# A channel's own input added on VectorE, with the gate, in place of a diagonal product in each sum

## The chip, the cores and the metric

The kernel runs on one core of a Trainium2 chip. The metric is the device time of one execution in microseconds (us), the median of a few runs. The core's engines have short names in the profile: PE is TensorE (matrix products; PEld is its weight loads), DVE is VectorE, ACT is ScalarE, POOL is GpSimd, and SP is the queue that starts the DMAs. They run side by side and wait for each other by semaphores. SBUF is the working memory of 128 partitions, PSUM holds the eight banks that TensorE sums into. All data are 32-bit floats.

## The reference, cut to what matters

Eight sequences of 512 tokens with 256 features pass two layers. The first (attention-like mixing and a mixture of experts) is not touched. The second has a state-space block and then a gated MLP. What the change touches is the end of the state-space block:

```python
h = jax.nn.silu(conv + conv_b)                    # 512 tokens x 512 channels
dA = jnp.exp(dt[..., None] * A)                   # 16 states for each channel
dBu = dt[..., None] * Bmat[:, :, None, :] * h[..., None]
# per token: state = dA * state + dBu ; y = sum over the 16 states of state * C
y = _ssm(dA, dBu, C)
y = y + h * D                                     # the channel's own input, one factor D for each channel
y = y * jax.nn.silu(gate)
return y @ W_out
```

## The kernel before, in words

The second layer works sequence by sequence (b = 0 to 7). 512 channels lie on 128 partitions in KI = 4 tiles (c = 0 to 3), the tokens along the free axis, so one tile of a quantity is 128x512. The scan over tokens is done for one state n and one channel tile c at a time: 16 x 4 = 64 steps s for each sequence. The first 32 steps (the first half) serve tiles 0 and 1 in turn, the last 32 serve tiles 2 and 3. One step is:

- ACT makes exp(dt*A) into one of three PSUM banks (line 1421, `bank<-dt,a_neg`), three steps ahead at most;
- POOL makes dt*h*B (line 1356, `d_in<-u,bc`), from rows `bc` that SP loads for every partition;
- DVE scans (line 1366, `bank<-bank,d_in`) and weighs the states with C (line 1374, `w_st<-bank,bc`);
- PE adds the weighed states to the tile's sum: a product with the identity into the tile's PSUM bank (line 1441, `bank<-w_st,ident`). A product of 32-bit floats runs as two passes, which the profile counts one by one.

The sum of a tile is opened by `begin_output(c)` (lines 1426 to 1433): a product of `skip_diag` (the factors D on a diagonal, made once at lines 497 to 499) with the tile's input `h`, which gives h*D. It waits until the bank has been read by the tile that used it before. After the last step of a half, `gate_output(c)` (lines 1377 to 1380) multiplies the bank by the gate into `hcv` (the buffer that held h), and PE later multiplies all four tiles by `w_out`.

Around this core three other sequences are under way: the front of sequence b+1 (norm, input products, convolution on DVE at lines 1188 and 1192, SiLU, and the step width dt, made by `make_dt` with Abs, Relu, Exp and Ln on ACT), and the MLP of sequence b-1. The MLP has eight up tiles, two hidden layers of eight tiles (PE lines 229 and 230, high and low parts of each operand), and a last product (lines 1674 and 1675). Its weights come by SP into `w_stage` (lines 1510 and 1515) and are cast by ACT into a ring `w_ring` of two slots (line 1597). In the up stage, a cast moves half a slot (128x512), in the hidden layers a whole one (128x1024); SP may load the next weights only when the cast before them is done.

The order of the instructions on each engine is written when the program is built. Each stage of work is a generator that yields a planned time before each piece, and `in_order` lines all stages up by these times, for each engine apart. The planned times are sums of the numbers in `PLAN`, in a model in which a step takes 2.8. They fix only the order; on the chip each engine runs its own list from top to bottom, and waits on semaphores. So an instruction that waits holds up everything behind it on its engine. `dt_first` places `make_dt(0)` on ACT, `up_cast_odd` places the casts of odd weight tiles in the up stage (and with it SP's loads two tiles on, by `mlp_sync`), and `last_add` places the last additions of the MLP on DVE (lines 1581 and 1584).

## Time and profile before

| what | us |
| --- | --- |
| median of 3 runs (2719.23 to 2723.3) | 2720.88 |
| the profiled execution: its own time | 2726.29 |
| the profiled execution: span from first to last instruction | 2724.6 |
| PE busy | 2330.2 |
| DVE busy | 1748.2 |
| ACT busy | 1505.2 |
| POOL busy | 1226.2 |

The span is the length that the rows show; the execution's own time is 1.7 us longer, since it also holds what lies before the first and after the last instruction. The profiled execution is 5.4 us longer than the median of the runs. In rows of time, the first number is the start in us from the span's start, the second the duration, and brackets at a row's end give how long the engine stood idle before it and what ended that. An instruction can start before the one ahead of it on its engine has ended, so starts follow each other more closely than durations.

The second layer begins near 990 us. From the second sequence on, the pattern repeats every 200 to 204 us.

### The profile page before, as it was taken

The page shows a single profiled execution, that of the slowest core. Times are in us where ns is not written, and L with a number is a line of the kernel's source. Part 1 is how long each engine was busy: PE and PEld are TensorE (multiplying, and loading weights), DVE is VectorE, ACT ScalarE, POOL GpSimd, SP SyncE. Part 2 cuts the span into 40 slices and gives each one's busy share as a digit, 9 for nine tenths or more (in the row PEclk, how much of TensorE's full clock was granted, in tenths as well). Part 3 has the DMA queues.
Part 4 walks back from the last instruction along what each step waited for, and adds up shares of the span by engine and source line. Part 5 has one row for each costly group of instructions (what it writes and reads, how often), then busy time and mean ns, then how long its engine had stood idle before and what let it go on. Part 6 is the DMA issues. An engine that isn't in the chain of part 4 may idle for free.

```text
span 2724.6 us, 27484 instructions
## 1 busy us (share of the span) xinstructions
PE 2330.2 (86%) x8452; PEld 1465.7 (54%) x8452; DVE 1748.2 (64%) x2782; ACT 1505.2 (55%) x1982; POOL 1226.2 (45%) x974
## 2 busy tenths in 40 slices
PE   2898989989989846778998998988988988998977
PEld 1456656567566622234554555555555555565666
DVE  3445464555454337899679679689689689687620
ACT  0232433425324225547877876876867866877733
POOL 1232251332422214556556556565556555556622
PEclk6899999999999867888999999998999999999988
DMA  7034534454445533444655645645645544647522
GB/s 227 0 119 137 166 124 133 150 162 132 136 137 155 174 110 108 119 117 131 171 133 131 170 133 134 171 132 129 175 129 134 171 128 138 160 133 176 151 83 78
DMA packets 381907, 374.34 MB, mean 137 GB/s; under 512 B 22369, under 2 KB 308593, under 8 KB 381761
## 3 DMA queue, kind: packets, MB, share of 16 engines
q1 hardware_dynamic: 375616, 355.80, 46.0%
q0 software_dynamic: 6144, 16.79, 2.0%
q8 instruction: 68, 1.11, 0.2%
q14 instruction: 79, 0.64, 0.1%
HBM read 335.45 MB, written 37.06 MB: 137 GB/s over the span
## 4 chain that ended last, share of the span: by engine, by line
PE 20%; DVE 13%; issue 11%; ACT 9%; DMA 6%; POOL 4%; SPq 1%; DVEq 0%; POOLq 0%; ACTq 0%
DMA w_stage<-h_T 5%; PE bank L1441 5%; PE bank L223 4%; DVE bank L1366 4%; PE bank L229 4%; PE bank L230 4%; DVE w_st L1374 4%; POOL d_in L1356 2%; ACT w_ring L1597 2%; ACT bank L1421 2%; DVE cv L1192 2%; ACT L1421 2%; PE bank L1674 1%; POOL f1L L1543 1%; PE bank L1675 1%
## 5 line engine op out<-in xcount | busy, mean ns | idle before, releaser
L1356 POOL TENSOR_TENSOR d_in<-u,bc 128x512 f32<-128x512 f32 x512 | 665.5, 1314 | 452.2 <-DMA bc<-bc_rows 327.7
L1366 DVE TENSOR_TENSOR_SCAN bank<-bank,d_in 128x512 f32<-128x512 f32 x512 | 624.7, 1221 | 185.7 <-ACT bank L1421 156.9
L1441 PE MATMUL bank<-w_st,ident 128*128 128x512 f32 x1024 | 544.8, 646 | 120.2 <-DVE w_st L1374 120.1
L1421 ACT ACTIVATE bank<-dt,a_neg 128x512 f32<-128x512 f32 x512 | 348.4, 687 | 292.9 <-DVE w_st L1374 291.0
L229 PE MATMUL bank<-f1H,w_ring 128*128 128x512 f32 x768 | 355.2, 462 | 34.8 <-POOL f1L L1543 23.8
L1441 PEld LDWEIGHTS bank<-w_st,ident 128*128 128x128 f32 x1024 | 194.2, 201 | 353.9 <-DVE w_st L1374 226.6
L1374 DVE TENSOR_TENSOR w_st<-bank,bc 128x512 f32<-128x512 f32 x512 | 343.9, 673 | 53.0 <-PE bank L1441 52.8
L230 PE MATMUL bank<-f1L,w_ring 128*128 128x512 f32 x768 | 311.3, 405 | 0.0
L229 PE MATMUL bank<-f0H,w_ring 128*128 128x512 f32 x512 | 230.2, 450 | 11.2 <-POOL f0L L1543 5.9
L1597 ACT ACTIVATE w_ring<-w_stage 128x1024 fp32r<-128x1024 f32 (+1 forms) x192 | 173.0, 905 | 112.6 <-DMA w_stage<-h_T 50.9
L1543 POOL TENSOR_TENSOR f0L<-mid,f0H 128x512 fp32r<-128x512 f32 x128 | 170.6, 1334 | 134.6 <-ACT f0H L1626 78.7
L193 POOL TENSOR_TENSOR norm_rstd<-norm_veps,minus_half 128x4 f32<-128x4 f32 x24 | 25.8, 1076 | 429.7 <-DVE norm_veps L189 429.5
L229 PEld LDWEIGHTS bank<-f1H,w_ring 128*128 128x128 f32 x768 | 151.4, 197 | 106.9 <-issue 43.2
L230 PE MATMUL bank<-f0L,w_ring 128*128 128x512 f32 x512 | 208.0, 406 | 0.0
L230 PEld LDWEIGHTS bank<-f1L,w_ring 128*128 128x128 f32 x768 | 151.3, 197 | 52.5 <-issue 23.8
L223 PE MATMUL bank<-f_both,w_s 128*128 128x512 f32 x256 | 140.0, 709 | 33.0 <-DVE s_act L867 33.0
L1421 ACT ACT_TABLE_LOAD x115 | 147.5, 1283 | 2.1
L1543 POOL TENSOR_TENSOR f1L<-mid,f1H 128x512 fp32r<-128x512 f32 x64 | 81.7, 1292 | 128.9 <-ACT f1H L1626 128.8
L223 PE MATMUL bank<-hT,w_in 128*128 128x512 f32 x256 | 125.5, 622 | 11.1 <-ACT f1H L1626 6.8
L229 PEld LDWEIGHTS bank<-f0H,w_ring 128*128 128x128 f32 x512 | 101.6, 199 | 56.2 <-POOL f0L L1543 16.8
L559 DVE TENSOR_REDUCE smax<-bank 128x1 f32<-128x512 f32 x32 | 22.1, 691 | 163.5 <-PE bank L223 163.5
L223 PE MATMUL bank<-e_buf,w_exp 128*128 128x128 f32 x960 | 120.4, 278 | 4.4 <-DMA w_exp<-L_ffn_ew 3.1
(202 smaller groups left out, 3898.5 us busy)
## 6 DMA issues: line engine op xcount, KB each, us to landing
bc<-bc_rows SPq DMA_DIRECT2D x256, 512.0 KB, 5.1
w_stage<-h_T SPq DMA_DIRECT2D x256, 256.0 KB, 3.4
w_exp<-L_ffn_ew SPq DMA_DIRECT2D x240, 256.0 KB, 4.6
w_stage<-w_T SPq DMA_DIRECT2D x128, 128.0 KB, 2.8
eo_rows<-eo SPq DMA_DIRECT2D x56, 256.0 KB, 4.3
xs<-xs_rows SPq DMA_DIRECT2D x24, 512.0 KB, 4.0
xA<-L_attn_x SPq DMA_DIRECT2D x8, 512.0 KB, 6.4
x_mid<-xA SPq DMA_DIRECT2D x8, 512.0 KB, 2.9
```

What stands on the lines that cost most here:

```text
L223: i = pe.matmul(out_, lhs(k), rhs(k), start=(k == 0), stop=(k == nk - 1))
L229: pe.matmul(out_, weights(k), hi(k), start=(k == 0), stop=False)
L230: i = pe.matmul(out_, weights(k), lo(k), start=False, stop=(k == nk - 1))
L1192: dve.scalar_tensor_tensor(out=o, in0=r[:, tap:tap + S], scalar=conv_w[:, tap, c:c + 1], in1=o, op0=ALU.mult, op1=ALU.add).then_inc(tap_ma ...
L1356: pool.tensor_tensor(d_in[:, nth(b, s) % IN, :], u[:, c, :], rows_tile(b, use)[:, 0, :], ALU.mult).then_inc(in_made.sem, 1)
L1366: dve.tensor_tensor_scan(bank[:, :], bank[:, :], d_in[:, nth(b, s) % IN, :], 0.0, ALU.mult, ALU.add).then_inc(scanned.sem, 1)
L1374: dve.tensor_tensor(w_st[:, nth(b, s) % WG, :], state_bank(b, s)[:, :], rows_tile(b, step(s)[2])[:, 1, :], ALU.mult).then_inc(weighed.sem, 1)
L1421: act.activation(state_bank(b, s)[:, :], dt[:, c, :], ACT.Exp, scale=a_neg[:, c, n:n + 1]).then_inc(dA_made.sem, 1)
L1441: pe.matmul(y_bank(c)[:, :], ident[:, :], w_st[:, nth(b, s) % WG, :], start=False, stop=(n == NST - 1)).then_inc(summed.sem, 1)
L1543: pool.tensor_tensor(lo, f_full[:, i % 2, :], hi.bitcast(F32), ALU.subtract).then_inc(low_made.sem, 1)
L1597: act.activation(ring_part(w), stage_part(w), ACT.Copy).then_inc(ring_made.sem, 1)
L1674: pe.matmul(bank[:, j * D:(j + 1) * D], f0H[:, k, token], w3[:, k, :], start=(k == 0), stop=False)
```

## The change

The diagonal product is gone, with `skip_diag`. The first step's product now opens the sum. `gate_output` gets one more DVE instruction: it reads the sum from the bank, adds `h` times D, and writes `y` to SBUF, and the gate is then multiplied in SBUF. The bank is free after the first of the two. `make_dt` loses a semaphore: Exp now waits for the last Relu where it waited for the last Abs. Three numbers of `PLAN` differ.

```diff
-    u_second=8.3, ... dt_first=107, dt_second=2.2,
+    u_second=8.3, ... dt_first=104.9, dt_second=2.2,
-    ... up_cast_even=-0.5, up_cast_odd=6.5, ...
+    ... up_cast_even=-0.5, up_cast_odd=0.5, ...
-    ... up_gate=6.5, last_add=1.5, m_act=9,
+    ... up_gate=6.5, last_add=2.6, m_act=9,
...
-                dve.wait_ge(ssm_weights_in.sem, 7 * 16)
-                for c in range(KI):
-                    dve.tensor_scalar(skip_diag[:, c, :], ident[:, :], d_skip[:, c:c + 1], None, ALU.mult)
...
-                        act.activation(cv[:, c % 2, :], bank[:, :], ACT.Abs, bias=b_dt[:, c:c + 1]).then_inc(abs_made.sem, 1)
+                        act.activation(cv[:, c % 2, :], bank[:, :], ACT.Abs, bias=b_dt[:, c:c + 1])
                         act.activation(dt[:, c, :], bank[:, :], ACT.Relu, bias=b_dt[:, c:c + 1]).then_inc(relu_made.sem, 1)
-                    act.wait_ge(*abs_made.at(b, HC * (half + 1)))
+                    act.wait_ge(*relu_made.at(b, HC * (half + 1)))
...
                 def gate_output(c):
                     dve.wait_ge(*summed.at(b, (c // HC + 1) * HALF))
+
+                    dve.scalar_tensor_tensor(out=y[:, c, :], in0=y[:, c, :], scalar=d_skip[:, c:c + 1], in1=y_bank(c)[:, :],
+                                             op0=ALU.mult, op1=ALU.add).then_inc(y_skipped.sem, 1)
                     dve.wait_ge(*gate_made.at(b, c + 1))
-                    dve.tensor_tensor(y[:, c, :], y_bank(c)[:, :], gate[:, c, :], ALU.mult).then_inc(y_gated.sem, 1)
+                    dve.wait_ge(*y_skipped.at(b, c + 1))
+                    dve.tensor_tensor(y[:, c, :], y[:, c, :], gate[:, c, :], ALU.mult).then_inc(y_gated.sem, 1)
...
                 def begin_output(c):
-                    if c < HC:
-                        pe.wait_ge(*h_made.at(b, c + 1))
-                        if b:
-                            pe.wait_ge(*y_gated.at(b - 1, c + HC + 1))
-                    else:
-                        pe.wait_ge(*y_gated.at(b, c - HC + 1))
-                    pe.matmul(y_bank(c)[:, :], skip_diag[:, c, :], h[:, c, :], start=True, stop=False)
+                    if c >= HC:
+                        pe.wait_ge(*y_skipped.at(b, c - HC + 1))
+                    elif b:
+                        pe.wait_ge(*y_skipped.at(b - 1, c + HC + 1))
...
-                    pe.matmul(y_bank(c)[:, :], ident[:, :], w_st[:, nth(b, s) % WG, :], start=False, stop=(n == NST - 1)
+                    pe.matmul(y_bank(c)[:, :], ident[:, :], w_st[:, nth(b, s) % WG, :], start=(n == 0), stop=(n == NST - 1)
```

What moves is seen in the engines' lists. First DVE, at the end of a sequence's 64 steps, in the steady part; line 1366 is a scan, 1374 a weighing, 1380 the gate, 1581 and 1584 the first of the MLP's two last additions, 1199 and 1204 make dt and u. Before:

```order
L1380 TENSOR_TENSOR hcv<-bank,gate 128x512 [waits gate_made,summed] x2
L1366 SCALAR_TENSOR_TENSOR bank<-bank,d_in 128x512 [waits dA_made,in_made] x2
L1374 TENSOR_TENSOR w_st<-bank,bc 128x512 [waits summed,scanned]
L1366 SCALAR_TENSOR_TENSOR bank<-bank,d_in 128x512 [waits dA_made,in_made]
L1374 TENSOR_TENSOR w_st<-bank,bc 128x512 [waits summed,scanned]
L1581 TENSOR_TENSOR mid<-bank,gbM 128x512 [waits g3_made,last_done]
L1584 TENSOR_TENSOR xM<-xM,mid 128x512 [waits last_scaled]
L1199 TENSOR_TENSOR dt<-dt,cv 128x1024 [waits relu_made,sp_ln]
L1204 TENSOR_TENSOR u<-dt,hcv 128x1024 [waits in_made,h_made,dt_made]
L1366 SCALAR_TENSOR_TENSOR bank<-bank,d_in 128x512 [waits dA_made,in_made]
L1374 TENSOR_TENSOR w_st<-bank,bc 128x512 [waits summed,scanned]
```

The same place now (the lines of the program have shifted by 4 or 3: 1362 is the scan, 1370 the weighing, 1376 the new instruction):

```order
L1376 SCALAR_TENSOR_TENSOR hcv<-hcv,d_skip,bank 128x512 [waits summed]
L1380 TENSOR_TENSOR hcv<-hcv,gate 128x512 [waits y_skipped,gate_made]
L1376 SCALAR_TENSOR_TENSOR hcv<-hcv,d_skip,bank 128x512 [waits summed]
L1380 TENSOR_TENSOR hcv<-hcv,gate 128x512 [waits y_skipped,gate_made]
L1362 SCALAR_TENSOR_TENSOR bank<-bank,d_in 128x512 [waits dA_made,in_made] x2
L1370 TENSOR_TENSOR w_st<-bank,bc 128x512 [waits summed,scanned]
L1362 SCALAR_TENSOR_TENSOR bank<-bank,d_in 128x512 [waits dA_made,in_made]
L1370 TENSOR_TENSOR w_st<-bank,bc 128x512 [waits summed,scanned]
L1578 TENSOR_TENSOR mid<-bank,gbM 128x512 [waits g3_made,last_done]
L1581 TENSOR_TENSOR xM<-xM,mid 128x512 [waits last_scaled]
L1195 TENSOR_TENSOR dt<-dt,cv 128x1024 [waits relu_made,sp_ln]
L1200 TENSOR_TENSOR u<-dt,hcv 128x1024 [waits in_made,h_made,dt_made]
```

Two instructions stand where the gate's two stood before, and two more; nothing else moves down to u. A little further on, the MLP's second pair of last additions stands behind one more scan and weighing than before (`last_add`), still ahead of the first `tokB`.

Second PE, at the middle of a sequence, where the sums of tiles 2 and 3 open; `hT,w_in` is an input product of the next sequence, `hcv,w_x` the product that gives B, C and the rows for dt. Before:

```order
L1441 MATMUL bank<-w_st,ident 128x512 [waits weighed]
L223 MATMUL bank<-hT,w_in 128x512 [waits h_act]
L223 MATMUL bank<-hT,w_in 128x512
L1433 MATMUL bank<-hcv,skip_diag 128x512 [waits y_gated]
L1441 MATMUL bank<-w_st,ident 128x512 [waits weighed]
L1433 MATMUL bank<-hcv,skip_diag 128x512 [waits y_gated]
L1441 MATMUL bank<-w_st,ident 128x512 [waits weighed]
L223 MATMUL bank<-hcv,w_x 96x512 [waits h_act,h_made]
L223 MATMUL bank<-hcv,w_x 96x512 x3
```

Now (1438 is the sum's product):

```order
L1438 MATMUL bank<-w_st,ident 128x512 [waits weighed]
L222 MATMUL bank<-hT,w_in 128x512 [waits h_act]
L222 MATMUL bank<-hT,w_in 128x512
L1438 MATMUL bank<-w_st,ident 128x512 [waits weighed,y_skipped] x2
L222 MATMUL bank<-hcv,w_x 96x512 [waits h_act,h_made]
L222 MATMUL bank<-hcv,w_x 96x512 x3
```

The two diagonal products are gone, and the sum's first products wait for the new DVE instruction.

Third ACT, right behind that place: `xp` is the copy of those rows, 1421 the exponential of a step, 1234 to 1239 make dt, 1597 is a cast of MLP weights. Before:

```order
L1272 ACTIVATE xp<-bank 96x512 [waits dt_done,bc_stored1,xp_done]
L1421 ACTIVATE bank<-dt,a_neg 128x512 [waits weighed] x2
L1234 ACTIVATE cv<-bank,b_dt 128x512 [waits u_made,dA_made,dt_done]
L1235 ACTIVATE dt<-bank,b_dt 128x512
L1234 ACTIVATE cv<-bank,b_dt 128x512 [waits u_made,dA_made,dt_done]
L1235 ACTIVATE dt<-bank,b_dt 128x512
L1237 ACTIVATE cv<-cv 128x1024 [waits abs_made]
L1239 ACT_TABLE_LOAD
L1239 ACTIVATE cv<-cv 128x1024 [waits sp_exp]
L1421 ACT_TABLE_LOAD
L1421 ACTIVATE bank<-dt,a_neg 128x512 [waits weighed]
L1597 ACTIVATE w_ring<-w_stage 128x1024 [waits h_done,stage_in1,stage_in0]
```

Now (1230 to 1235 make dt, 1594 is the cast):

```order
L1268 ACTIVATE xp<-bank 96x512 [waits dt_done,bc_stored1,xp_done]
L1421 ACTIVATE bank<-dt,a_neg 128x512 [waits weighed]
L1230 ACTIVATE cv<-bank,b_dt 128x512 [waits u_made,dA_made,dt_done]
L1231 ACTIVATE dt<-bank,b_dt 128x512
L1230 ACTIVATE cv<-bank,b_dt 128x512 [waits u_made,dA_made,dt_done]
L1231 ACTIVATE dt<-bank,b_dt 128x512
L1233 ACTIVATE cv<-cv 128x1024 [waits relu_made]
L1235 ACT_TABLE_LOAD
L1235 ACTIVATE cv<-cv 128x1024 [waits sp_exp]
L1421 ACT_TABLE_LOAD
L1421 ACTIVATE bank<-dt,a_neg 128x512 [waits weighed] x2
L1594 ACTIVATE w_ring<-w_stage 128x1024 [waits h_done,stage_in1,stage_in0]
```

One exponential has moved from ahead of dt to behind it (`dt_first`). In the up stage of the MLP, each cast of an odd weight tile stands right behind the even one's, or one exponential behind it, where it stood some six units of the plan later (`up_cast_odd`): the cast of tile 3 is ahead of the first SiLU, those of tiles 5 and 7 each ahead of the SiLU that they followed, and the loads of the weights on SP move up with them, past one load of `bc` rows and the store of the result.

## Rows read from the trace of the kernel before

**Rows 1.** The page: busy time of the engines, and shares of the chain that ended last.
```profile
PE 2330.2 (86%) x8452; PEld 1465.7 (54%) x8452; DVE 1748.2 (64%) x2782; ACT 1505.2 (55%) x1982; POOL 1226.2 (45%) x974
...
PE 20%; DVE 13%; issue 11%; ACT 9%; DMA 6%; POOL 4%; SPq 1%; DVEq 0%; POOLq 0%; ACTq 0%
```

**Rows 2.** Windows: stretch and length in us, busy us of PE, PEld, DVE, ACT, POOL (instructions), PE clock, DMA.
```profile
1799.00:1877.00 78.00, 67.13 (x239) 41.36 (x237) 76.93 (x106) 52.02 (x69) 42.64 (x33) 0.93 0.46 117
1747.00:1798.00 51.00, 49.90 (x171) 32.97 (x172) 34.77 (x39) 40.60 (x52) 35.51 (x29) 0.97 0.61 166
1708.00:1744.00 36.00, 34.77 (x110) 20.28 (x110) 19.77 (x23) 32.44 (x42) 16.55 (x14) 1.00 0.61 174
```

**Rows 3.** All waits of VectorE from 1799 to 1877 us: total, times, longest.
```profile
DVE tokB L1405 <- PE bank L223: 0.3, 1, 0.3
```

**Rows 4.** The chain of waits where a sequence's steps end: start, us, what.
```profile
1801.93 0.86 PE bank L1433 x2
```

**Rows 5.** VectorE in order of time, where the second layer starts.
```profile
986.48 0.87 DVE L499 TENSOR_SCALAR skip_diag<-ident,d_skip 128x128 f32<-128x128 f32 x4
993.74 0.43 DVE L181 BATCH_NORM_STATS2 normB_stat<-xB 128x6 f32<-128x256 f32 x1 [6.39 <-DMA xB<-x_mid]
```

**Rows 6.** VectorE in order of time, from the end of a sequence's steps.
```profile
1798.06 1.29 DVE L1380 TENSOR_TENSOR hcv<-bank,gate 128x512 f32<-128x512 f32 x2 [5.29 <-PE bank L1441]
1799.26 2.33 DVE L1366 TENSOR_TENSOR_SCAN bank<-bank,d_in 128x512 f32<-128x512 f32 x2
...
1812.68 0.69 DVE L1405 TENSOR_TENSOR tokB<-bank,gaB 128x512 f32<-128x512 f32 x1
1813.40 0.69 DVE L1408 TENSOR_TENSOR xM<-xM,tokB 128x512 f32<-128x512 f32 x1
1814.01 1.23 DVE L1366 TENSOR_TENSOR_SCAN bank<-bank,d_in 128x512 f32<-128x512 f32 x1
```

**Rows 7.** VectorE, 1799 to 1877 us, groups: count, busy us, mean ns, idle us.
```profile
L1192 DVE SCALAR_TENSOR_TENSOR cv<-raw,conv_w,cv 128x512 f32<-128x512 f32 x6 | 6.4, 1064 | 0.0
...
L198 DVE TENSOR_SCALAR cv<-xB,normB_stat,normB_rstd 128x256 f32<-128x256 f32 x4 | 4.5, 1178 | 0.0
L1564 DVE SCALAR_TENSOR_TENSOR mid<-bank,sc_in,mid 128x512 f32<-128x512 f32 x6 | 4.4, 736 | 0.0
```

**Rows 8.** VectorE in the last sequence, 38 us behind the same place.
```profile
2443.95 1.23 DVE L1366 TENSOR_TENSOR_SCAN bank<-bank,d_in 128x512 f32<-128x512 f32 x1 [1.51 <-POOL d_in L1356]
```

**Rows 9.** VectorE behind the middle of a sequence.
```profile
1715.37 1.23 DVE L1366 TENSOR_TENSOR_SCAN bank<-bank,d_in 128x512 f32<-128x512 f32 x1 [5.39 <-ACT bank L1421]
```

**Rows 10.** TensorE at the middle of a sequence.
```profile
1710.37 1.02 PE L1433 MATMUL bank<-hcv,skip_diag 128*128 128x512 f32 x2
...
1713.80 3.60 PE L223 MATMUL bank<-hcv,w_x 128*96 128x512 f32 x8
1718.08 1.98 PE L223 MATMUL bank<-xp,w_dt 64*128 64x512 f32 x4 [0.68 <-ACT xp L1272]
```

**Rows 11.** ScalarE at the middle of a sequence.
```profile
1710.96 1.33 ACT L1216 ACTIVATE hcv<-cv,conv_b 128x512 f32<-128x512 f32 x2
...
1715.81 1.04 ACT L1597 ACTIVATE w_ring<-w_stage 128x1024 fp32r<-128x1024 f32 x1
1717.43 0.59 ACT L1272 ACTIVATE xp<-bank 96x512 f32<-96x512 f32 x1 [0.58 <-PE bank L223]
...
1718.93 0.69 ACT L1421 ACTIVATE bank<-dt,a_neg 128x512 f32<-128x512 f32 x1 [0.33 <-DVE w_st L1374]
```

**Rows 12.** ScalarE in the last MLP, where the hidden layers begin.
```profile
2624.54 1.06 ACT L1597 ACTIVATE w_ring<-w_stage 128x1024 fp32r<-128x1024 f32 x1 [0.72 <-DMA w_stage<-h_T]
```

**Rows 13.** The convolution's instruction over the whole span: shortest, median, longest in ns.
```profile
L1192 DVE SCALAR_TENSOR_TENSOR cv<-raw,conv_w,cv x96: 731/746/1870, 1007.5 to 2306.8; 128x512 f32<-128x512 f32 x96
```

**Rows 14.** GpSimd in order of time, where a sequence's steps end.
```profile
1800.63 2.54 POOL L1356 TENSOR_TENSOR d_in<-u,bc 128x512 f32<-128x512 f32 x2 [2.84 <-DVE bank L1366]
```

**Rows 15.** The norm's application over the whole span, columns as in rows 13.
```profile
L198 DVE TENSOR_SCALAR cv<-xB,normB_stat,normB_rstd x32: 400/1347/1503, 997.0 to 2242.6; 128x256 f32<-128x256 f32 x32
```

More of the change, by code:

```diff
@@ L27 @@
     rows_out=106.9, norm_rstd=29, norm_stats=26, norm_apply=34.2, conv=45.7, raw_gap=11.7, tap_gap=3, u_first=136.5,
-    u_second=8.3, hT_act=36.9, raw_act=42.3, h_first=66, h_second=97, rows_act=102, dt_first=107, dt_second=2.2,
+    u_second=8.3, hT_act=36.9, raw_act=42.3, h_first=66, h_second=97, rows_act=102, dt_first=104.9, dt_second=2.2,
     gate_second=23.1, turn=35.2, raw_pe=38.6, gate_pe_first=92, rows_pe=100, dt_pe_first=98, dt_pe_second=-5.4,
     gate_pe_second=17, rows_in=3.3, input=3.2, weigh=-10.6, out_add=13.6, decay=3.7, sum=5.6, out_pe=10.8, up_gap=9,
-    hid_gap=13.8, mlp=20, up=14, hid=3.6, up_cast_even=-0.5, up_cast_odd=6.5, hid_cast_even=8, hid_cast_odd=12.6,
-    stage=3.1, m_rstd=1.9, m_low=10.9, up_low=11.6, hid_low=10.5, m_apply=5, up_gate=6.5, last_add=1.5, m_act=9,
+    hid_gap=13.8, mlp=20, up=14, hid=3.6, up_cast_even=-0.5, up_cast_odd=0.5, hid_cast_even=8, hid_cast_odd=12.6,
+    stage=3.1, m_rstd=1.9, m_low=10.9, up_low=11.6, hid_low=10.5, m_apply=5, up_gate=6.5, last_add=2.6, m_act=9,
     up_act=2.2, hid_act=8, m_turn=3.3, up2_pe=1.3, hid_pe_odd=3.5, last_pe=-1.1)
@@ L162, in adaln_kernel @@
         a_neg = keep("a_neg", [P, KI, NST])
-        skip_diag = keep("skip_diag", [P, KI, P])
         s3_row = keep("s3_row", [P, D])
@@ L1091, in adaln_kernel @@
             xp_done, xp_made = signal("xp_done"), signal("xp_made")
-            dt_done, abs_made, relu_made = signal("dt_done", KI), signal("abs_made", KI), signal("relu_made", KI)
+            dt_done, relu_made = signal("dt_done", KI), signal("relu_made", KI)
             sp_exp, sp_ln, dt_made, u_made = (signal(n, HALVES) for n in ("sp_exp", "sp_ln", "dt_made", "u_made"))
@@ L1096, in adaln_kernel @@
                                                           ("dA_made", "in_made", "scanned", "weighed", "summed"))
-            y_gated = signal("y_gated", KI)
+            y_skipped, y_gated = signal("y_skipped", KI), signal("y_gated", KI)
             so_done, so_gated, xM_made = (signal(n, 2) for n in ("so_done", "so_gated", "xM_made"))
```

## The prediction

> **What bounds the kernel now.** I began with the page's busy times and chain shares [rows 1]: TensorE is busy for 86% of the span and VectorE for 64%, yet TensorE holds only 20% of the chain that ended last, and VectorE 13%. So no one engine sets the time. I then cut one steady sequence into stretches and read the busy time of each engine in each [rows 2], with the waits beside it. Three stretches come out.
>
> In the first, some 78 us from the end of a sequence's 64 steps, VectorE works 76.93 of 78 us, and its waits there come to 0.3 us in all [rows 3]; TensorE has 11 us to spare. Here each instruction that VectorE gains moves the end. The same stretch stands at the start of each of the seven sequences that follow another.
>
> The second stretch is the middle of a sequence with the first hidden layer behind it: TensorE works 34.77 of 36 us and ScalarE 32.44, while VectorE works 19.77. The third is the second hidden layer: TensorE works 49.90 of 51 us, up to the end of the steps.
>
> So the change takes from TensorE, which binds in the second and third stretch, and gives to VectorE, which binds in the first. What counts is where the removed and the added instructions stand: a pair at the end of each sequence, ahead of a VectorE-full stretch, and a pair at its middle, in the second stretch. None stands in the third.
>
> **What is removed.** The two passes of a diagonal product take 0.86 us on the chain [rows 4], so 0.43 us a pass. There are 8 sequences with 4 products of two passes: 64 x 0.43 = 27.5 us of TensorE's work, 1.72 us for each of the 16 pairs. If all of it shortened the chain, the time would fall by 27.5 us: the lower bound. Making `skip_diag` took 0.87 us once. It goes at no gain, because VectorE next waits 6.39 us for a load [rows 5], which waits for a store that does not need it. The moved wait for Relu in place of Abs costs nothing: Relu follows Abs on the same engine, and the Exp that waits is behind both on it.
>
> **What is added.** Two gates start the next instruction 1.20 us later (1798.06 to 1799.26), so 0.60 us each; two independent instructions on VectorE start 0.61 us apart (1813.40 to 1814.01), and one that reads the last one's result starts 0.72 us behind it (1812.68 to 1813.40) [rows 6]. The new instruction is of the form scalar_tensor_tensor with one input in PSUM and one in SBUF, like line 1564's, which takes 736 ns where a plain one takes 690 [rows 7, 6]. I take 0.72 + 0.05 = 0.77 us from its start to that of the gate that waits for it, and 0.61 from there to the next. A pair takes 2 x (0.77 + 0.61) = 2.76 us in place of 1.20: 1.56 us more. For 16 pairs that is 25 us of VectorE's work, and if all of it lengthened the chain, it would be the upper bound.
>
> **At a sequence's end (seven times).** The pair ends 1.56 us later, and the scan behind it starts later. Of that, the stretch's 0.3 us of waits can absorb 0.3 [rows 3], so 1.26 us reach its end. The 1.72 us saved on TensorE bring nothing here: the diagonal products stood where TensorE was waiting for VectorE's first weighing anyway, since a scan and a weighing follow the gates. Now TensorE waits 1.7 us there instead, and the bank's earlier release serves a sum that is not ready. In the last such stretch VectorE waits 1.51 us for GpSimd [rows 8]; that can hold most of the 1.56, and I put 0.3 there. Sum: 6 x 1.26 + 0.3 = +7.9 us. Behind the eighth sequence there is no such stretch, and the last MLP hides the pair. That pair and the place of the last additions (the MLP's second pair goes behind one scan and one weighing, all within the same full stretch, and TensorE waits for none of it there) I put at 0.
>
> **At a sequence's middle (eight times).** VectorE's 1.56 us are covered: a few instructions on, a scan waits 5.39 us for an exponential [rows 9]. If that cover were gone, they would cost 1.56 each. TensorE reaches `w_x` 1.72 us earlier, but that product needs h, which ScalarE makes at 1710.96 + 1.33 = 1712.29; it starts now at 1713.80 [rows 10, 11], so it can gain 1.51. Its reader, the copy `xp`, now waits 0.58 us behind a cast that ends at 1815.81 + 1.04 = 1816.85 (and starts at 1717.43), so `xp` can gain 0.58. Behind it an exponential with a wait of 0.33 us goes behind dt [rows 11], where its operand is long ready: 0.33 more at best, 0.91 in all, and then TensorE's dt products, which wait 0.68 us for `xp` today [rows 10], follow. At worst it is 0, since the casts and loads of the hidden layer run behind one another. I take 0.4, near the middle: 8 x 0.4 = -3.2 us.
>
> **Casts and loads moved ahead in the up stage.** SP's weight loads pass one load of `bc` rows and a store, and ScalarE's casts pass a SiLU. In the steady sequences they lie in the VectorE-full stretch, where ScalarE works 52.02 of 78 us [rows 2]; I put 0. In the last MLP, ScalarE waits 0.72 us for a load where the hidden layers begin [rows 12]; an earlier load can take that, -0.7 us, and 0 at worst.
>
> **The sum.** 7.9 - 3.2 - 0.7 = +4.0 us. The profiled execution took 2726.3 us, so it becomes 2730.3; the median of the runs is 5.4 us lower, and so is the forecast: 2724.9, called 2725.
>
> **A rule that speaks against the change.** The convolution's instruction reads two operands in SBUF and takes 731 ns when alone, up to 1870 when not [rows 13]. The old gate read PSUM and SBUF; the new one reads `hcv` and `gate`, both in SBUF. The Trainium skill ("SBUF — State Buffer", section "Who interferes with whom") says that a VectorE instruction with two SBUF inputs contends with a GpSimd instruction that reads SBUF, the second to come blocking for the whole of the other, and that one with a single SBUF input does not. By that rule the trace's 731 and 1870 agree, and the new gate would be exposed where the old one was not. With one GpSimd product of 1.27 us waited for at each of the seven ends the sum would be +4.0 + 8.9 = +12.9 us by the rule, and +4.0 without it.
>
> **The rivals.**
> *Slower: the new gate collides.* A product of GpSimd takes 2.54 / 2 = 1.27 us, and just ahead of 1800.63 GpSimd idles for 2.84 us [rows 14], so the gates at 1798 to 1800.8 start in its idle time; that speaks against a collision. But VectorE's new schedule is 1.56 us longer, so its last gate reaches the point where GpSimd starts again, unless GpSimd, which waits for VectorE's scan there, moves along. With one collision of 1 us at each of seven ends: +7, so 2732. From 0.2 us per end the time is above the bound of no change.
> *Faster: fewer collisions.* Within a VectorE-full stretch the convolution's six instructions take 1064 ns against 731 alone, and the norm's four 1178 against 400 [rows 7, 13, 15]: 6 x 0.33 + 4 x 0.78 = 5.1 us lost per stretch, 36 us over seven. These depend on which instructions meet, and the moved gates, loads and casts lay all of them anew. A third less would be -12 us: 2713. A third more is equally open in principle; the slower rival and the range hold it.
> *Faster: TensorE is the true bound at the middle.* It works 34.77 of 36 us there. If h were early and each pair's 1.72 us came through in full, 8 x 1.72 = 13.8 in place of 3.2 gives 2725 - 10.6 = 2714. Against it stands the order h, `w_x`, `xp`, in which ScalarE's cast sets the start.
> *Slower: adjacent casts hold ScalarE.* Two casts in a row wait for a load that has only just been asked for, and the exponentials behind them are late. ScalarE has 26 us to spare in each VectorE-full stretch, which speaks against it; it decides from the point where VectorE's scans wait for an exponential there. With 1.4 us, two exponentials of 0.69, at each of seven sequences: +10, 2735.
>
> **How the numbers follow.** A difference below 0.2%, 5.4 us, cannot be told from no change for this kernel; the bounds are 2715.4 and 2726.3. The forecast gets 0.44 (its own range 2719 to 2731: 0.05 faster, 0.24 same, 0.15 slower), fewer collisions 0.20 (0.15 faster, 0.05 same), TensorE at the middle 0.13 (0.10, 0.03), the gate's collision 0.15 (0.02 same, 0.13 slower), the casts 0.08 (0.01, 0.07). Together: faster 0.30, same 0.35, slower 0.35. The range that leaves out 2 in 10 reaches from 2709 to 2737.
>
> **What the profile of the changed kernel would show.** Right: 32 new instructions near 0.74 us and 32 gates near 0.69; the first scan 2.76 us behind the first of them at a sequence's end; TensorE waiting some 1.7 us for the first weighing there; still hardly a wait on VectorE in the 78 us behind; a period per sequence longer by about 0.9 us. Wrong: gates above 0.75 us (the collision); the convolution's mean in that stretch far from 1064 ns (the other collisions); the period shorter with TensorE's waits at the middle unchanged (TensorE was the bound); casts with waits of over 1 us in the up stage.

## The result, and the profile after

The changed kernel takes 2737.29 us (median of 4 runs, 2733.26 to 2742.31), beside 2720.12 us of the kernel before on the same chip: ratio 1.0062, 95% interval 1.0043 to 1.0081. It is slower, by three times the 0.2% that the prediction took as the least difference that can be told. The forecast was 2725 us; the measured time lies at the upper end of the stated range (2737), 0.3 us beyond it, and on the side to which the prediction gave a chance of 0.35. The forecast was 4 us of change and 17 were measured: that the time comes so near the range is due to the range, which was held open for collisions that no term priced.

From the page of the changed kernel: span and instructions, busy times, shares of the chain that ended last.

```profile
span 2731.5 us, 27400 instructions
...
PE 2298.4 (84%) x8388; PEld 1447.5 (53%) x8388; DVE 1776.5 (65%) x2810; ACT 1505.9 (55%) x1982; POOL 1236.6 (45%) x974
...
PE 17%; DVE 16%; issue 11%; ACT 9%; DMA 7%; POOL 3%; SPq 1%; DVEq 0%; POOLq 0%; ACTq 0%
```

TensorE has 64 passes fewer than before and works 32 us less; VectorE has 28 instructions more (32 added, the four of `skip_diag` gone) and works 28 us more [rows 1]. VectorE's 28 us are not the price of the change alone: the added instructions take 23.8 us, the gates 2.8 more than before and the MLP's norm 11.2 more, while one group of the first layer (`qk_tok<-qk_tok,os_row_t`), which the change does not touch, happens to take 10.1 less in this trace. TensorE's share of the chain fell from 20 to 17%, VectorE's rose from 13 to 16%.

The spans of the two profiled executions differ by only 6.9 us, where the medians differ by 17. One row shows where the rest is: VectorE's first instruction of the second layer.

```profile
983.72 1.40 DVE L180 BATCH_NORM_STATS2 normB_stat<-xB 128x6 f32<-128x256 f32 x4 [7.17 <-DMA xB<-x_mid]
```

In the execution of before it started at 993.74 [rows 5], 10 us later, though ahead of it the change took out only the 0.87 us of `skip_diag`. From that instruction to the end the kernel before took 2724.6 - 993.7 = 1730.9 us, the changed one 2731.5 - 983.7 = 1747.8: 16.9 us more, close to the difference of the medians. The traces are therefore compared by this length, called "layer 2" below; a trace is one execution, a verdict rests on the runs.

The three stretches (columns as in [rows 2]), and all waits of VectorE in the first of them:

```profile
1799.00:1880.00 81.00, 64.84 (x226) 39.43 (x225) 79.42 (x108) 51.90 (x67) 44.11 (x34) 0.94 0.44 112
1747.00:1796.00 49.00, 47.70 (x169) 31.59 (x170) 34.52 (x39) 39.51 (x51) 35.23 (x29) 1.00 0.62 172
1708.00:1744.00 36.00, 33.90 (x106) 19.36 (x106) 21.69 (x25) 32.69 (x43) 17.24 (x14) 1.00 0.60 176
```

```profile
DVE tokB L1405 <- PE bank L222: 0.9, 2, 0.6
```

The first stretch, as I cut it, grew from 78 to 81 us and VectorE is as full as it was (76.93 of 78 before [rows 2]). The second, at a sequence's middle, holds 0.9 us less of TensorE's work, and the third, up to the end of the steps, is 49 us long in place of 51; they did not become the problem.

To see where in a sequence the time is lost, I took the start of every scan (steps 0 to 63) and compared each kernel with the one before, averaged over the sequences 1 to 6. A positive number is us lost between the two steps, and step 64 is the next sequence's first. Steps 0 to 12 hold the MLP's last additions and its norm, 32 to 40 the middle, 60 to 64 the gates at the end:

```
kernel                     0-12  12-32  32-40  40-60  60-64   whole
changed kernel              1.8   -0.5    1.3   -1.5    1.7     2.8
casts put back (e1)         1.7   -0.2    0.9   -1.4    1.5     2.5
arithmetic only (e2)        0.3   -0.1    0.2   -0.3    1.4     1.4
order only (e3)             2.1    0.3    1.4   -1.1   -0.3     2.4
last_add only (e8)          1.8    0.2    0.4   -0.3   -0.1     2.0
no product, no sum (e4)     0.1   -0.7    0.2    0.0   -0.3    -0.7
tiles 0, 1 on VectorE (e5)  0.2    0.2    0.0   -0.4   -0.3    -0.4
tiles 2, 3 on VectorE (e6)  0.3    0.2    0.4   -0.3    1.5     2.2
in first weighed (e7)       0.0    0.3    1.0    0.0   -0.1     1.2
extra work at end (e9)      2.1   -0.3    0.0    0.1    2.9     4.7
extra work at middle (e10)  0.7   -0.2    0.2   -0.2   -0.2     0.3
last_add put back (e11)     2.3    0.7    0.9   -0.9    1.3     4.2
both covered (e12)         -0.3    0.1    0.0    0.7   -0.3     0.1
```

The changed kernel loses 2.8 us per sequence: 1.7 at the end's gates and 1.8 at the norm, and between step 12 and 60 it gains 0.7.

**The end.** VectorE in order of time, the place of [rows 6]:

```profile
1796.86 0.75 DVE L1376 SCALAR_TENSOR_TENSOR hcv<-hcv,d_skip,bank 128x512 f32<-128x512 f32 x1 [5.40 <-PE bank L1438]
1797.71 0.69 DVE L1380 TENSOR_TENSOR hcv<-hcv,gate 128x512 f32<-128x512 f32 x1
1798.32 0.74 DVE L1376 SCALAR_TENSOR_TENSOR hcv<-hcv,d_skip,bank 128x512 f32<-128x512 f32 x1
1799.17 0.69 DVE L1380 TENSOR_TENSOR hcv<-hcv,gate 128x512 f32<-128x512 f32 x1
1799.78 2.34 DVE L1362 TENSOR_TENSOR_SCAN bank<-bank,d_in 128x512 f32<-128x512 f32 x2
```

The first scan starts 2.92 us behind the first added instruction; before, it stood 1.20 us behind the first gate. The added instruction takes 0.75 us (forecast: near 0.74), but what waits for it starts 0.85 us behind it, not 0.77. TensorE now waits for the first weighing, 2.19 us where some 1.7 were forecast:

```profile
1802.84 1.32 PE L1438 MATMUL bank<-w_st,ident 128*128 128x512 f32 x2 [2.19 <-DVE w_st L1370]
```

**The norm.** VectorE, GpSimd and SP where the MLP's norm is applied, in the kernel before. The three fences are the three engines; SPq rows are DMAs that SP issues.

```profile
1824.62 1.80 DVE L198 TENSOR_SCALAR mid<-xM,normM_stat,normM_rstd 128x256 f32<-128x256 f32 x4
1826.34 1.22 DVE L1366 TENSOR_TENSOR_SCAN bank<-bank,d_in 128x512 f32<-128x512 f32 x1
```

```profile
1824.04 1.26 POOL L1356 TENSOR_TENSOR d_in<-u,bc 128x512 f32<-128x512 f32 x1
1826.62 2.50 POOL L1356 TENSOR_TENSOR d_in<-u,bc 128x512 f32<-128x512 f32 x2 [1.31 <-DMA bc<-bc_rows]
```

```profile
1820.76 0.88 SPq L1510 DMA_DIRECT2D w_stage<-w_T  x2
1821.68 10.56 SPq L1335 DMA_DIRECT2D bc<-bc_rows  x3
```

The same in the changed kernel:

```profile
1825.74 3.69 DVE L197 TENSOR_SCALAR mid<-xM,normM_stat,normM_rstd 128x256 f32<-128x256 f32 x4
1829.36 1.22 DVE L1362 TENSOR_TENSOR_SCAN bank<-bank,d_in 128x512 f32<-128x512 f32 x1
```

```profile
1825.16 3.80 POOL L1352 TENSOR_TENSOR d_in<-u,bc 128x512 f32<-128x512 f32 x3
```

```profile
1813.74 0.46 SPq L1331 DMA_DIRECT2D bc<-bc_rows  x1
...
1818.53 7.69 SPq L1331 DMA_DIRECT2D bc<-bc_rows  x2
```

Before, SP asks for the `bc` rows at 1821.68. They arrive 4.94 us later, so GpSimd stands idle until 1826.62, and by then the norm's four instructions are over: they end at 1826.42. That is a gap of 0.2 us; in the sequences 2 to 6 GpSimd starts from 0.3 us ahead of the norm's end to 0.4 behind it. In the changed kernel the rows were asked for at 1818.53, 7.2 us ahead of the norm in place of 2.9; GpSimd runs three products on end, and the four instructions take 3.69 us in place of 1.80. Over the whole span, shortest, median and longest in ns:

```profile
L198 DVE TENSOR_SCALAR mid<-xM,normM_stat,normM_rstd x32: 399/402/1451, 1217.6 to 2602.6; 128x256 f32<-128x256 f32 x32
```

```profile
L197 DVE TENSOR_SCALAR mid<-xM,normM_stat,normM_rstd x32: 400/830/1348, 1210.6 to 2612.9; 128x256 f32<-128x256 f32 x32
```

The sum over the group's 32 instructions goes from 17.9 to 29.1 us, 11.2 us more, all of it in VectorE-full stretches. The first of the four takes 0.83 us at every end in both kernels. What is new is that the second and third take 1.35 us each: in the kernel before at one of seven ends, in the changed one at all seven. In the sequences 1 to 6 that makes 1.9 us for each, as much as step 0 to 12 loses.

**The middle** went as forecast in its rows. In this sequence the middle's first gate instruction starts at the same time in both traces (1706.97 us before, 1706.98 now), so the times can be compared as they stand: `xp` on ScalarE no longer waits for TensorE and stands 0.66 us earlier (1717.43 to 1716.77), and Abs on dt's rows 1.0 us earlier (1719.56 to 1718.56) [rows 11]. Two rows of ScalarE, two of VectorE:

```profile
1716.77 0.57 ACT L1268 ACTIVATE xp<-bank 96x512 f32<-96x512 f32 x1
...
1718.56 0.69 ACT L1230 ACTIVATE cv<-bank,b_dt 128x512 f32<-128x512 f32 x1 [0.64 <-PE bank L222]
```

```profile
1709.28 1.12 DVE L1380 TENSOR_TENSOR hcv<-hcv,gate 128x512 f32<-128x512 f32 x1
...
1715.37 1.23 DVE L1362 TENSOR_TENSOR_SCAN bank<-bank,d_in 128x512 f32<-128x512 f32 x1 [3.26 <-ACT bank L1421]
```

The second gate of the pair takes 1.12 us here, where an operation of GpSimd still runs (`f1L<-mid,f1H`, two of them from 1708.58 to 1711.52), and 0.69 at the end. VectorE then still waits 3.26 us, so the longer gate is covered. From step 12 to 60 the changed kernel gains 0.7 us in sum.

### The profile page after: what moved, and what is told of

It reads as the page before. It is cut to its first block, busy times and chain, and to the rows that moved or that the text cites. A ratio compares the mean times of both kernels' runs of the same rounds, so it can differ in the third digit from the quotient of the medians.

```text
span 2731.5 us, 27400 instructions
## 1 busy us (share of the span) xinstructions
PE 2298.4 (84%) x8388; PEld 1447.5 (53%) x8388; DVE 1776.5 (65%) x2810; ACT 1505.9 (55%) x1982; POOL 1236.6 (45%) x974
## 4 chain that ended last, share of the span: by engine, by line
PE 17%; DVE 16%; issue 11%; ACT 9%; DMA 7%; POOL 3%; SPq 1%; DVEq 0%; POOLq 0%; ACTq 0%
DMA w_stage<-h_T 6%; PE bank L1438 5%; DVE bank L1362 5%; DVE w_st L1370 4%; PE bank L228 4%; PE bank L229 4%; PE bank L222 3%; POOL d_in L1352 2%; ACT w_ring L1594 2%; ACT bank L1421 2%; ACT L1421 2%; DVE cv L1188 2%; POOL f1L L1540 1%; DVE mid L197 1%; DVE mid L1561 1%
```

## The experiments

Ratios are to the kernel before on the same chip, with 95% intervals. The diffs are against the kernel before, unless said otherwise.

**e1, one number of the plan put back in the changed kernel.**

```diff
-    up_cast_odd=0.5
+    up_cast_odd=6.5
```

> The changed kernel with one number of the plan put back (up_cast_odd 6.5). Theory 1: with the casts moved ahead, SP asks for the bc rows about 3 us sooner, GpSimd's products of that stretch then run while VectorE applies the MLP's norm, and two of its four instructions take 1.35 us instead of 0.40; 11 us of the 17 us lost are this. Then the four take 0.83, 0.40, 0.40, 0.40 again (the group's sum falls from 29 to about 18 us) and the time is near 2726 us, ratio to before 1.002. Theory 2: the collision comes from the 1.5 us by which VectorE is late behind the two added instructions, whatever SP does; then the sum stays near 29 us and the time near 2737, ratio 1.006.

Measured: 2745.84 us, ratio 1.0074 [1.0058, 1.0090]. The norm's instructions stay long (their sum is 27.2 us):

```profile
L197 DVE TENSOR_SCALAR mid<-xM,normM_stat,normM_rstd x32: 400/829/1349, 1221.5 to 2622.7; 128x256 f32<-128x256 f32 x32
```

Theory 1 as I put it falls: the moved casts alone are not the cause. Theory 2 (VectorE's lateness) would explain it, and e2 and e3 decide on it.

**e2, the change without the three numbers of the plan.** The diff is against the changed kernel.

```diff
-    dt_first=104.9 ... up_cast_odd=0.5 ... last_add=2.6
+    dt_first=107 ... up_cast_odd=6.5 ... last_add=1.5
```

> The change without the three numbers of the plan. Theory 1: the same as with the casts alone put back, 2726 us, ratio 1.002, made of seven ends of a sequence at 1.1 to 1.4 us each less 3 us at the middles. Theory 2: 2737 us, ratio 1.006. If dt_first and last_add were worth something of their own, this run stands above the one with only the casts put back, by their worth.

Measured: 2739.07 us, ratio 1.0052 [1.0036, 1.0069]; layer 2 1741.6 us, +10.8.

```profile
L197 DVE TENSOR_SCALAR mid<-xM,normM_stat,normM_rstd x32: 399/402/1349, 1218.4 to 2615.7; 128x256 f32<-128x256 f32 x32
```

The median is 402 ns again, the sum 19.7 us. So VectorE's lateness does not make the collision at five of the seven ends (at the last two it is there): theory 2 falls in the main, and the collision comes from the order. The time hardly falls, though: the arithmetic alone still costs 0.52%, 1.4 us at each end.

**e3, the order without the arithmetic.** The diff is e2's in reverse, on the kernel before.

> The kernel before with the three new numbers of the plan, the diagonal product kept. Theory 1: the norm's application meets GpSimd's products here too, +11 us, near 2731, ratio 1.004. Theory 2: no collision without the added VectorE work: 2718 to 2721, ratio 1.000 or a little below.

Measured: 2739.30 us, ratio 1.0049 [1.0032, 1.0065], layer 2 +11.8. The group's sum is 29.1 us:

```profile
L198 DVE TENSOR_SCALAR mid<-xM,normM_stat,normM_rstd x32: 401/832/1350, 1221.6 to 2618.9; 128x256 f32<-128x256 f32 x32
```

The order alone costs as much as the arithmetic alone, and it costs it at the norm (2.1 us from step 0 to 12). The two do not add up to the changed kernel: 0.52% and 0.49% against 0.62% [0.43, 0.81]. The table has the place. Between step 12 and 60 the changed kernel gives back 0.7 us per sequence, where e2 gives back 0.2 and e3 loses 0.6, so 1.1 us are there only when both are made; in the other columns the differences cancel. The rows at the middle point the same way: e2 has `xp` 0.66 us earlier and dt where it was, e3 has `xp` as before and dt 0.3 us earlier, and only both together have dt 1.0 us earlier. That this is the cause of the whole 1.1 us is not shown.

**e4, no diagonal product, and nothing in its place** (h*D is left out of the result).

```diff
-                    pe.matmul(y_bank(c)[:, :], skip_diag[:, c, :], h[:, c, :], start=True, stop=False)
...
-                    pe.matmul(..., start=False, stop=(n == NST - 1)
+                    pe.matmul(..., start=(n == 0), stop=(n == NST - 1)
```

> The kernel before without the diagonal product and with nothing in its place: h*D is left out of the result. It prices TensorE's 27.5 us alone. As forecast: nothing at the ends of a sequence, where TensorE waits for VectorE, and 0.4 us at each middle: 2717, ratio 0.999. Rival, TensorE is the bound at the middle: 1.72 us each, 2706, ratio 0.995. The lower bound, all of it on the path: 2693.

Measured: 2716.16 us, ratio 0.9960 [0.9945, 0.9974]. The 27.5 us of TensorE are worth about 11 us, between my value and the rival's; the trace shows -6.0 in layer 2. In this order of the instructions it is what a way of doing this sum off TensorE could bring if VectorE's part cost nothing.

**e5, tiles 0 and 1 on VectorE** (the pair at the middle), **e6, tiles 2 and 3 on VectorE** (the pair at the end). The plan is before's; only the set differs:

```diff
+ON_VECTOR = (0, 1)      # e6: (2, 3)
...
+                    if c in ON_VECTOR:
+                        dve.scalar_tensor_tensor(out=y[:, c, :], in0=y[:, c, :], scalar=d_skip[:, c:c + 1], in1=y_bank(c)[:, :], ...)
...
+                    if c not in ON_VECTOR:
                         pe.matmul(y_bank(c)[:, :], skip_diag[:, c, :], h[:, c, :], start=True, stop=False)
```

> Before's plan; tiles 0 and 1 get h*D on VectorE with the gate (the pair at a sequence's middle), tiles 2 and 3 keep the diagonal product. Theory 'the place decides': the added pair lies under VectorE's wait of 5 us at the middle, so it costs nothing, and the product that goes stood at the end of a sequence, where TensorE waits: 0 to -5 us, 2720 to 2726 beside 2725 of before, ratio 0.998 to 1.000. Rival 'every added instruction counts': half of the 14 us of the arithmetic alone, ratio 1.0026.

> The other half: tiles 2 and 3 get h*D on VectorE (the pair at a sequence's end, ahead of the VectorE-full stretch), tiles 0 and 1 keep the diagonal product. Theory 'the place decides': all of the cost of the arithmetic alone is here, +12 to +15 us, ratio 1.0045 to 1.0055. Rival: half of it, ratio 1.0026.

Measured: e5 2722.86 us, ratio 0.9981 [0.9964, 0.9997]; e6 2732.85 us, ratio 1.0019 [1.0005, 1.0032]. The signs are those of "the place decides": the pair at the middle costs nothing, and e5's interval leaves out the rival's 1.0026; the pair at the end does cost. The size of e6 is short of what was expected, +5 us in the runs and not 12 to 15: its interval leaves out the expected 1.0045 and holds the rival's 1.0026, so e6 alone does not decide between the two. Its own trace has layer 2 14.4 us longer and 1.5 us lost at each end as in e2, but the profiled execution is the slowest of its twelve (2741.07 us; they spread over 14 us). In the traces the halves add up to the whole (-4.4 and +14.4 us in layer 2, e2 +10.8); in the runs they do not (-0.19% and +0.19%, e2 +0.52%). Why is open; e9 and e10 test the place with more weight.

**e7, h*D added to the first weighed states.** Tiles 2 and 3 only, at the middle; the gates stay as before.

```diff
+                    dve.tensor_tensor(w, state_bank(b, s)[:, :], rows_tile(b, step(s)[2])[:, 1, :], ALU.mult ...)
...
+                    if first:
...
+                        dve.scalar_tensor_tensor(out=w, in0=y[:, c, :], scalar=d_skip[:, c:c + 1], in1=w, ...)
```

> Before's plan; for tiles 2 and 3 h*D is added on VectorE to the first weighed states, right at a sequence's middle, where VectorE has idle time, and TensorE's product for them goes; tiles 0 and 1 keep the diagonal product, which stands where TensorE waits. The gates stay as before. If the place decides, this has TensorE's gain at the middle and none of VectorE's cost at the end: 2718 to 2724 beside 2725, ratio 0.997 to 0.9995. If the first weighed states come too late for TensorE by the added 0.75 us each, 1.000 to 1.002.

Measured: 2733.58 us, ratio 1.0026 [1.0013, 1.0039]. It is slower: the "too late" branch, and a little beyond it. Shortest, median and longest of the added instruction:

```profile
L1382 DVE SCALAR_TENSOR_TENSOR w_st<-hcv,d_skip,w_st x16: 750/752/1662, 1118.2 to 2506.2; 128x512 f32<-128x512 f32 x16
```

It reads two operands in SBUF and takes up to 1.66 us. It stands on the way from scan to sum, and 1.0 us per sequence is lost from step 32 to 40, though less work is asked of TensorE there.

**e8, last_add alone.**

```diff
-    last_add=1.5
+    last_add=2.6
```

> The kernel before with last_add 2.6 and nothing else. In the run with the casts put back (where the collision stayed) one weighing stands ahead of the MLP's last addition, and SP asked for the bc rows 4.98 us ahead of the norm's application where it was 2.94 before, so GpSimd's products ran beside it. If last_add does that, the group of the MLP's norm takes 27 to 29 us here instead of 18, and the time is 7 to 11 us above before: ratio 1.0025 to 1.004. If it takes dt_first or the added instructions as well, the group stays at 18 and the ratio at 1.000.

Measured: 2733.99 us, ratio 1.0026 [1.0012, 1.0040]; the group's sum is 27.2 us. VectorE at the norm, GpSimd, SP:

```profile
1829.21 3.69 DVE L198 TENSOR_SCALAR mid<-xM,normM_stat,normM_rstd 128x256 f32<-128x256 f32 x4
```

```profile
1828.63 3.80 POOL L1356 TENSOR_TENSOR d_in<-u,bc 128x512 f32<-128x512 f32 x3
```

```profile
1822.60 0.88 SPq L1510 DMA_DIRECT2D w_stage<-w_T  x2
1823.53 6.17 SPq L1335 DMA_DIRECT2D bc<-bc_rows  x2
```

One number that moves a weighing ahead of an addition lets SP ask for the rows 5.7 us ahead of the norm (1823.53 to 1829.21) and no longer 2.9; nothing else in the kernel differs. The weighing acts on that ask through SP's queue, in two steps. An earlier `bc` load (1812.57 before, 1815.84 in e8) waits for the weighing that frees its buffer, 7.2 us before and 5.8 in e8; the weight load that stands ahead of the ask waits for a cast of weights that came in behind that `bc` load, 5.0 us before and 2.1 in e8. From the second end on, the ask comes 21.6 to 22.4 us behind the sequence's first scan in the kernel before, 19.6 to 21.2 in e8 and 18.1 to 18.8 in the changed kernel.

The traces of the two kernels, e1, e2, e3, e8 and e11 hold 49 ends of a sequence. Where SP asked 4.6 us or more ahead of the norm, the second and third instruction of the norm took about 1.35 us, every time; where it asked 3.6 us or less ahead, never; the one end between (3.7, in the kernel before) has them too. That settles the mechanism: the norm was spared this only because GpSimd was short of its rows at that moment.

**e9, more work at each end; e10, the same at each middle.** The gate is computed three times. Both kernels also let Exp wait for Relu in place of Abs, as the change does, and use that semaphore for the repeated gates (not in the cut below):

```diff
+                    if c in (2, 3):     # e10: (0, 1)
+                        for i in range(2):
+                            dve.tensor_tensor(y[:, c, :], y_bank(c)[:, :], gate[:, c, :], ALU.mult).then_inc(again.sem, 1)
+                            dve.wait_ge(*again.at(b, 2 * (c % HC) + i + 1))
```

> Before's arithmetic and plan; at each sequence's end the gate of tiles 2 and 3 is computed three times in place of once, each waiting for the one ahead of it: 4 more VectorE instructions of 0.72 us, 2.9 us per end, about 1.7 times what the change adds there. Theory 'VectorE's time at the end is on the path': 7 x 2.9 = 20 us less what waits absorb, so +15 to +20 us, ratio 1.0055 to 1.0075. Rival 'the loss is in the alignment, not in the added time': under +7 us, ratio under 1.0025.

> The same four extra instructions at each sequence's middle (tiles 0 and 1), 2.9 us in each of eight places, ahead of a wait of VectorE of 5.4 us. As forecast the wait covers them: 0 to +3 us, ratio 1.000 to 1.001. Rival 'every added instruction counts': +20 us, ratio 1.0075.

Measured: e9 2754.89 us, ratio 1.0100 [1.0077, 1.0122], so +27 us; e10 2730.34 us, ratio 1.0008 [0.9993, 1.0023], not to be told from nothing. VectorE at an end in e9:

```profile
1812.62 1.42 DVE L1382 TENSOR_TENSOR hcv<-bank,gate 128x512 f32<-128x512 f32 x2 [5.38 <-PE bank L1445]
1814.07 0.69 DVE L1384 TENSOR_TENSOR hcv<-bank,gate 128x512 f32<-128x512 f32 x1
1814.68 1.41 DVE L1382 TENSOR_TENSOR hcv<-bank,gate 128x512 f32<-128x512 f32 x2
1816.12 0.69 DVE L1384 TENSOR_TENSOR hcv<-bank,gate 128x512 f32<-128x512 f32 x1
1816.73 2.34 DVE L1366 TENSOR_TENSOR_SCAN bank<-bank,d_in 128x512 f32<-128x512 f32 x2
```

The first scan starts 4.11 us behind the first gate, 2.91 us more than before. In the table the end loses 2.9 us, which is all of it, and another 2.1 us go by step 12: the norm's four instructions take 0.9 us more per sequence (the group has grown by 5.3 us over the span), and `tokB` waits 0.9 us more for TensorE. So VectorE's time at an end is paid in full, with 1.8 us per sequence on top; at a middle the runs show no cost. This is the clearest of the results.

**e11, the changed kernel with last_add put back.**

```diff
-    last_add=2.6
+    last_add=1.5
```

> The changed kernel with last_add put back to 1.5; the casts stay ahead. If last_add alone makes GpSimd's products meet the MLP's norm, the group of the norm falls from 29 to about 18 us and the ratio to before to 1.003 to 1.005. If the casts ahead do it too (SP then asks for the bc rows without waiting for a cast), it stays at 27 to 29 us and the ratio at 1.005 to 1.0065.

Measured: 2750.11 us, ratio 1.0078 [1.0054, 1.0103].

```profile
L197 DVE TENSOR_SCALAR mid<-xM,normM_stat,normM_rstd x32: 400/830/1350, 1224.9 to 2636.1; 128x256 f32<-128x256 f32 x32
```

The collision stays, at all seven ends, though this kernel's `last_add` is that of before. With e8, either of the two moves, the last additions or the casts and loads, brings the rows in time for it. (e11 also keeps `dt_first`, which no run tests alone.) And with one of them put back the changed kernel is no faster (e1, e11).

**e12, both additions where VectorE has idle time.** e5, and for tiles 2 and 3 e7's addition in their eleventh step, in the second hidden layer; no diagonal product is left.

```diff
+                    late = n == 10 and c >= HC
```

> Before's plan, no diagonal product at all. Tiles 0 and 1 get h*D with the gate at the middle, tiles 2 and 3 get it in the weighed states of their eleventh step, in the second hidden layer, where VectorE works 34.77 of 51 us and TensorE is full. The gates at a sequence's end stay as before. If TensorE's time is worth what leaving the product out gave (ratio 0.996) and both places are covered: 2716 to 2720 beside 2726, ratio 0.996 to 0.998. If the two added instructions delay the sums as they did in the first weighed states, 1.000 to 1.002.

Measured: 2730.61 us, ratio 1.0015 [1.0000, 1.0031].

```profile
L1382 DVE SCALAR_TENSOR_TENSOR w_st<-hcv,d_skip,w_st x16: 750/767/1614, 1172.4 to 2556.8; 128x512 f32<-128x512 f32 x16
```

From step 40 to 60 it loses 0.7 us per sequence, and the whole comes to +0.1 where leaving the product out gave -0.7 (e4). My reading is that VectorE's idle time in that stretch is waiting inside the chain of scan, weighing and sum, so an instruction put between two links makes what follows late; the two of 0.75 us cost 0.7 us together, and no run tests them apart.

The version that is faster than the kernel before is e5, by 0.2% [0.0, 0.4]: it moves h*D of tiles 0 and 1 only.

## Why the prediction was right or wrong

- **That the place decides what VectorE's time costs:** right, and shown. e9 and e10 put the same 2.9 us at either place: +1.00% and +0.08%.
- **The added pair, +1.56 us:** 1.72 us. What depends on the new instruction starts 0.85 us behind it. No wait absorbs a part of it (VectorE's waits are 0.9 us in that stretch in place of 0.3). So 1.7 us come through where the forecast had 1.26, some 3 us over seven ends; in e2 it is 1.4.
- **"The 1.72 us saved on TensorE bring nothing here":** doubtful. Leaving all products out gains 0.40% (e4), which is 11 us where my terms for the product hold 3.2, so 8 us are missing; whether they come from the ends or the middles, e4 does not tell. In e5 it is this product that goes, and the kernel gains 0.19%, but e5 also puts h*D of the middle's pair on VectorE, which changes when those banks come free, so it doesn't isolate the product.
- **The middle, -3.2 us:** the step is right in its rows (`xp`'s wait of 0.58 us gone, dt 1.0 us earlier), and 0.7 us per sequence are gained between steps 12 and 60, against 0.4 forecast. The prediction writes the cast's start there as 1815.81 and its end as 1816.85; the row has 1715.81 [rows 11], so the end is 1716.85. The 0.58 is read from the row's bracket and stands.
- **"That pair and the place of the last additions (...) I put at 0":** this is the step that failed, together with the zero for the casts and loads moved ahead in the steady sequences. Moving one weighing ahead of an addition costs 0.26% alone (e8), the three numbers 0.49% (e3). The reason given, that all lies in the same full stretch and TensorE waits for none of it, looked at the wrong reader. The weighing frees a buffer for a `bc` load of SP, the loads behind that one in SP's queue come sooner, and the next `bc` load sets when GpSimd runs beside VectorE's norm. The 11.2 us at the norm are most of the distance between the forecast's +4.0 us and the measured +17.
- **The rivals:** of the collisions the prediction had the size and the mechanism (5.1 us lost per stretch, laid anew by the moves), but gave a chance only to fewer of them, and left more of them to the range. It named the convolution and the norm of `xB`. The one that came is that of the MLP's norm, which had it at one of seven ends before and was in none of the rows that I read. The gate's own collision came about at the middle (1.12 us), where it is covered, and not at the end. That adjacent casts hold up VectorE's scans does not show in the stretch read: VectorE waits 0.9 us in all of it, for TensorE.

The Trainium skill ("SBUF — State Buffer", section "Who interferes with whom") says more than I used: one SBUF input keeps a VectorE instruction clear of GpSimd only outside the modes that use two ports, and tensor_scalar is among the operations that can enter such a mode. The trace agrees that the form is exposed: the norm's instruction, with one large SBUF input, takes 0.40 us alone and 1.35 us when it falls behind the start of a GpSimd product of 1.3 us.

## What to carry to other kernels

Price an instruction by its place: the same 2.9 us of VectorE's work cost 27 us over the kernel in front of a stretch in which VectorE is full, and nothing that the runs can tell in front of a wait. When the order is touched, follow each moved instruction to the buffer that it frees, to the load that waits for the buffer, and to the engine that the load wakes; then look at what that engine will run beside. An instruction that is fast in the trace may be so by a few tenths of a microsecond of luck, and a list of what would be slow if its neighbour came earlier belongs in the range.

## What the hardware showed that I had not expected

- A dependent VectorE instruction behind the three-operand form started 0.85 us after it (1796.86 to 1797.71), where behind a plain two-operand one it was 0.72 [rows 6].
- The first layer took 983.7 to 998.1 us to VectorE's first instruction of the second in the traces of these kernels, with almost the same instructions. A span compared between two single executions is uncertain by that much.
- The runs of one kernel spread over 6 to 20 us in the later comparisons, and those of before over 4 us in the first; with a dozen runs the intervals are still 0.3% wide.
